# A fused conv-attention and routed-feed-forward kernel: the first routed step gets its own copy of the code, and TensorE gets products of zeros in three places

## The chip, the cores and the metric

The kernel runs on one core of a Trainium2 chip. The metric is the device time of one execution in microseconds (us). Before the change it is 262.25 us, the median of three runs (262.20 to 262.34). The core has engines that run their own instruction streams and meet at semaphores: TensorE (PE; PEld is its weight load), VectorE (DVE), ScalarE (ACT), GpSimd (POOL) and SyncE (SP, which here issues DMAs).

## The reference

The input x is 4 x 64 x 32 x 32, fp32. Two blocks follow each other, each with a residual addition.

1. x += conv attention of the channel norm of x: for each pixel, softmax over its 7 x 7 neighbourhood of q.k plus a relative bias, then the weighted sum of v.
2. t += the routed block of the token norm of t, with 4096 tokens as 4 batches of 1024:

```
def step(h, p):
    op = argmax(h[0, 0, :NOPS])
    q, k, v = h @ wq[op], h @ wk[op], h @ wv[op]
    y = (softmax(q k^T * scale) v) @ wo[op]
    h = where(am[op], y, h)
    z = relu(h @ w1[op] + b1[op]) @ w2[op] + b2[op]
    h = where(fm[op], z, h)
out = scan(step, x, 33 steps)
```

Both masks am and fm depend on the step and on op, and op on the data. A step with both masks off leaves h as it is. Step 0 has fm on and am off for every op.

## The kernel before, in words

**Conv part (0 to 95 us).** Sixteen blocks of queries are worked off in a software pipeline in a loop: scores, exponentials, transposes and the mix. It is not touched.

**Second norm (89 to 105 us).** The tokens are four chunks of 512 columns, j = 0 to 3. For each chunk `centre(j)` (TensorE, L334) subtracts the mean; `square` on ScalarE writes the squares and copies the centred chunk (L708, L710); `variance(1, j)` is four small products on TensorE (L343); `root` on ScalarE (L714) and `inverse` on VectorE (L960) make the reciprocal deviation; `spread(1, j)` (TensorE, L352) spreads it over the partitions; `scale` on VectorE (L966) writes the chunk of h2 and raises `h_ready`. Two rules tie the chunks: `variance(1, j)` with j of 2 or more waits for `h_ready` of j - 1, and each engine works in the order of its program. On TensorE that order is centre(3), variance(1,1), spread(1,0), spread(1,1), variance(1,2), then `load_next()` of the routing, then variance(1,3), spread(1,2), spread(1,3).

**Routing.** Every engine but GpSimd has the same routing code. `load_next` (L176 to L190) waits for the decided op, reads it and a table entry into registers (two register loads, L181 and L184, and arithmetic), and so knows the next step that does anything, with its two masks am and fm. `run` (L207) is a loop over such steps. Each turn is an event: an If on am around `attention`, an If on fm around `feed_forward` (both in `section`, L194), and `load_next`. When a mask is 0, the compare-and-branch of L194 is taken and jumps over the body. In this input there are two events: a feed-forward alone, then attention with a feed-forward.

**feed_forward on TensorE (L651).** For the chunks t = 0 to 3, `up(t, c)` is two products of 64 rows by 512 columns side by side (L660), c = 0 and 1 for the halves of the hidden layer; ScalarE and VectorE each apply bias and relu to one half (L898, L1188); `down(t)` is four products (L674); ScalarE stores the chunk to h2 (L904), after it has also waited for `summed` of 4, that is for GpSimd's four additions of x and h2 (L322) that follow the norm; VectorE adds up (L1195). The order is up(0,0), up(0,1), up(1,0), up(1,1), down(0), up(2,1), up(2,0), down(1), the transposed row of the next decision, up(3,1), up(3,0), down(2), down(3). up(0,*) needs the first chunk of h2, up(1,*) waits for all four.

**attention on TensorE (L529).** Folded weights (L537, L539), `twice(0)` (L546), `queries` (L556), `twice(1)` (L546), then `tile_scores(0)` and `tile_scores(1)` (L582), `values` (L563), and from there 32 tiles in a pipeline of scores, exponentials (L832), transposes (L594) and mixes (L608). tile_scores(0) and (1) wait for parts that ScalarE and VectorE split off after `twice` (L813, L1094). ScalarE copies the values out of PSUM at L824.

`idle_in` is a tile of zeros. Before the change it is used for five products at the very start (L359, L367).

Of the kernel before, what the change touches and what calls it, by code (L numbers as in the profile page):

```python
# [24 lines left out]
ALU = mybir.AluOpType  # L25
# [3 lines left out]
P = 128  # L29
# [25 lines left out]
def build(nc, x, w_qk, w_q, w_v, bias_tables, key_onehot, masks, ident, mean_mat, spread_mat, iotas,  # L55
          attn_mask, ffn_mask, attn_pack, ffn_w1, ffn_pack, out):
    with ExitStack() as ctx:
# [96 lines left out]
        def routing(eng):  # L154
# [9 lines left out]

            name = eng.engine.name
            op, entry, step, cur, last, stride, am, fm, n_att, n_ffn, event = (
                eng.alloc_register(f"{name}_{k}")
                for k in "op entry step cur last stride am fm n_att n_ffn event".split())
            for reg in (n_att, n_ffn, event, cur):  # L170
                eng.reg_mov(reg, 0)

# [3 lines left out]
            def load_next():  # L176
# [12 lines left out]
                eng.reg_add(cur, step, 1)  # L189
                eng.reg_alu(cur, cur, NB, op=ALU.min)  # L190

            def run_event(attention, feed_forward):
                def section(mask, work, done):
                    with eng.If(eng.snap(mask, min_val=0, max_val=2) > 0):  # L194
                        work(eng.snap(n_att, min_val=0, max_val=NB),
                             eng.snap(n_ffn, min_val=0, max_val=NB),
                             eng.snap(event, min_val=0, max_val=NB),
                             eng.snap(eng.snap(step, min_val=0, max_val=NB - 1) * NOPS
                                      + eng.snap(op, min_val=0, max_val=NOPS - 1)))
                        eng.reg_add(done, done, 1)  # L200

                section(am, attention, n_att)
                section(fm, feed_forward, n_ffn)
                eng.reg_add(event, event, 1)
                load_next()

            def run(attention, feed_forward):  # L207
                eng.reg_mov(last, step)

                with eng.Fori(step, NB, stride):
                    run_event(attention, feed_forward)
                    eng.reg_alu(stride, step, last, op=ALU.subtract)
                    eng.reg_mov(last, step)
# [116 lines left out]
        def _(pe):  # L331
# [5 lines left out]
            def variance(k, j):  # L337

                pe.wait_ge(S["squared"], 4 * k + j + 1)
                if j >= 2:  # L340
                    pe.wait_ge(S["h_ready" if k else "normed"], j - 1)
                for s in range(4):
                    mm = nc.tensor.matmul(ps[32 * s:32 * s + 32, 4 + 2 * (j % 2), 0:P], mean_w[:, P:P + 32],  # L343
                                          sq[:, j * 512 + P * s:j * 512 + P * s + P], start=True, stop=True)
                mm.then_inc(S["var_ready"], 1)

            def spread(k, j):

                pe.wait_ge(S["inv_ready"], 4 * k + j + 1)
                for odd in range(2):  # L350
                    for r in range(2):
                        mm = nc.tensor.matmul(ps[:, 4 + 2 * (j % 2) + r, P * odd:P * odd + P],  # L352
                                              spread_w[C * r:C * r + C, odd, :],
                                              sq[C * r:C * r + C, j * 512:j * 512 + P], start=True, stop=True)
                mm.then_inc(S["spread_ready"], 1)

            pe.wait_ge(S["idle_set"], 1)
            for i in range(3):
# [156 lines left out]
            pe.wait_ge(S["mixed"], NPAIR)  # L515
            centre(3)
            variance(1, 1)
            spread(1, 0)
            spread(1, 1)
            variance(1, 2)  # L520
            load_next, run, sections = routing(pe)
            load_next()
# [6 lines left out]
            def attention(a, f, ev, row):  # L529
# [87 lines left out]
                pe.wait_ge(S["fold_a"], a + 1)  # L617
                queries(0, 0)
                twice(1, 6)
                tile_scores(0)  # L620
                tile_scores(1)
                pe.wait_ge(S["fold_d"], a + 2)
# [671 lines left out]
```

## Time and profile before

| | us |
|---|---|
| median of three runs | 262.25 |
| the profiled execution | 261.88 |
| its span, first to last instruction | 260.0 |
| TensorE busy in the span | 230.6 |
| VectorE, ScalarE, GpSimd busy | 170.7, 160.2, 39.5 |
| mean granted TensorE clock, share of full | 0.954 |

In the timelines a row is: start, duration, engine, line, operation, what is written and read, shapes, count, and in brackets the idle time before it with what ended it. Instructions that only an engine's sequencer works off (branches, register loads) are not in timelines or busy times; the view by source line names them with a q behind the engine, PEldq for TensorE's sequencer.

### The profile page before, as it was taken

How to read it: one execution, taken by the hardware profiler on the slowest of the kernel's cores; microseconds unless marked ns; L12 is line 12 of the kernel's file. 1: busy time of each engine (PE TensorE's matmuls, PEld its weight loads, DVE VectorE, ACT ScalarE, POOL GpSimd, SP SyncE). 2: the span in 40 equal slices, each digit the busy share in tenths (PEclk: the TensorE clock that was granted, in tenths of full speed). 3: DMA queues.
4: the chain of work that ended last, by engine and by line, in shares of the span. 5: the costliest groups of instructions: out<-in, count | busy, mean ns of one | idle time of the engine just before them, and what ended most of it. 6: DMA issues, size and time to landing. Idle time of an engine off the chain costs nothing.

```text
span 260.0 us, 5251 instructions
## 1 busy us (share of the span) xinstructions
PE 230.6 (89%) x1794; PEld 156.5 (60%) x1795; DVE 170.7 (66%) x312; ACT 160.2 (62%) x297; POOL 39.5 (15%) x66
## 2 busy tenths in 40 slices
PE   7879963999999996499869999999999999998992
PEld 3247623787777744233247687887877777777320
DVE  0279937677778736146385999898687666871652
ACT  1928753366666784045456997879877776663541
POOL 9800042454444100700000000000000000000000
PEclk9999997799999996579989999999999999999999
DMA  6850000000000010000100000000000000000006
GB/s 167 186 108 1 4 0 1 0 3 0 0 0 0 0 31 0 10 0 3 43 0 0 3 0 0 3 0 3 0 3 0 3 0 3 0 3 0 0 16 149
DMA packets 3304, 4.80 MB, mean 18 GB/s; under 512 B 1041, under 2 KB 2257, under 8 KB 3282
## 3 DMA queue, kind: packets, MB, share of 16 engines
q1 hardware_dynamic: 2758, 3.86, 6.6%
q10 hardware_dynamic: 524, 0.64, 1.1%
q8 instruction: 15, 0.25, 0.4%
q14 instruction: 7, 0.06, 0.1%
HBM read 3.45 MB, written 1.05 MB: 17 GB/s over the span
## 4 chain that ended last, share of the span: by engine, by line
PE 75%; ACT 9%; DVE 7%; issue 6%; ACTq 2%; POOL 0%; DVEq 0%; POOLq 0%
PE ps L594 11%; PE ps L608 11%; PE ps L582 8%; PE ps L660 7%; PE ps L435 7%; PE ps L674 6%; PE ps L467 5%; PE ps L456 5%; ACT arena L883 4%; PE ps L446 2%; PE ps L410 2%; PE ps L334 2%; PE ps L563 2%; DVE arena L996 2%; PE ps L352 2%
## 5 line engine op out<-in xcount | busy, mean ns | idle before, releaser
L883 ACT COPY arena<-ps 128x1024 f32<-128x1024 f32 x32 | 32.4, 1011 | 20.4 <-PE ps L594 19.4
L582 PE MATMUL ps<-h_st,g_st 128*128 128x512 f32 x128 | 39.5, 431 | 2.6 <-DVE h_st L1094 2.3
L1107 DVE TENSOR_REDUCE negmax<-ps 128x1 f32<-128x1024 f32 x32 | 38.7, 1219 | 3.8 <-PE ps L582 3.6
L832 ACT ACTIVATE pr<-ps,negmax 128x1024 f32<-128x1024 f32 x32 | 35.8, 1119 | 4.0 <-DVE negmax L1107 3.7
L594 PE MATMUL ps<-eye,pr 128*128 128x128 f32 x256 | 33.7, 275 | 2.7 <-ACT arena L883 2.3
L594 PEld LDWEIGHTS ps<-eye,pr 128*128 128x128 f32 x256 | 28.6, 140 | 11.1 <-issue 5.0
L608 PE MATMUL ps<-arena,vk 128*64 128x128 f32 x512 | 31.5, 276 | 1.1 <-ACT arena L883 1.1
L608 PEld LDWEIGHTS ps<-arena,vk 128*64 128x64 f32 x512 | 27.6, 137 | 3.8 <-issue 2.3
L766 ACT ACTIVATE prob<-ps,negmax 128x308 f32<-128x308 f32 x32 | 16.3, 513 | 21.0 <-DVE negmax L1007 21.0
L582 PEld LDWEIGHTS ps<-h_st,g_st 128*128 128x128 f32 x128 | 22.2, 193 | 11.3 <-DVE h_st L1094 3.5
L1117 DVE TENSOR_SCALAR pr<-pr,rinv 128x1024 f32<-128x1024 f32 x32 | 24.1, 753 | 1.1
L435 PE MATMUL ps<-arena,q_st 128*128 (+1 forms) x64 | 20.7, 446 | 1.7 <-POOL q_st L295 1.7
L660 PE MATMUL ps<-h,w1d 64*128 64x512 f32 x64 | 18.4, 712 | 3.4 <-issue 3.4
L898 ACT ACTIVATE arena<-ps,w2p 128x512 f32<-128x512 f32 x16 | 11.0, 688 | 15.1 <-PE ps L660 15.1
L1007 DVE TENSOR_REDUCE negmax<-ps 128x2 f32<-128x616 f32 x16 | 12.8, 799 | 7.4 <-PE ps L435 7.4
L456 PE MATMUL ps<-eye,prob 128*103 128x128 f32 x96 | 14.4, 286 | 2.9 <-DVE prob L1015 2.9
L1188 DVE TENSOR_SCALAR arena<-ps,w2p 128x512 f32<-128x512 f32 x16 | 11.6, 746 | 7.1 <-PE ps L660 6.9
L295 POOL TENSOR_TENSOR q_st<-arena,ones_c 128x128 f32<-128x128 f32 x32 | 12.2, 402 | 24.3 <-ACT arena L758 22.5
L776 ACT COPY prob_t<-ps 103x384 f32<-103x384 f32 x32 | 13.7, 481 | 3.1 <-PE ps L456 2.4
L302 POOL TENSOR_TENSOR v_st<-arena,ones_c 128x308 f32<-128x308 f32 x16 | 11.2, 701 | 25.9 <-PE ps L446 25.9
L674 PE MATMUL ps<-arena,w2p 128*64 128x512 f32 x64 | 15.1, 602 | 0.0
L1114 DVE RECIPROCAL rinv<-rowsum 128x1 f32<-128x1 f32 x32 | 5.1, 161 | 14.8 <-ACT pr L832 14.2
(110 smaller groups left out, 335.7 us busy)
## 6 DMA issues: line engine op xcount, KB each, us to landing
arena<-in_key_onehot SPq DMA_DIRECT2D x4, 361.0 KB, 6.2
out<-tabs SPq DMA_DIRECT2D x8, 128.0 KB, 2.3
x<-in_x SPq DMA_DIRECT2D x2, 256.0 KB, 3.9
x<-in_x ACTq DMA_DIRECT2D x2, 256.0 KB, 5.2
w1d<-in_ffn_w SPq DMA_DIRECT2D x4, 64.0 KB, 2.1
w2p<-in_ffn_pack SPq DMA_DIRECT2D x2, 65.5 KB, 1.9
spread_w<-in_spread_mat SPq DMA_DIRECT2D x4, 32.0 KB, 5.0
mean_w<-in_mean_mat SPq DMA_DIRECT2D x1, 96.0 KB, 2.1
```

Source lines behind the costliest of these rows:

```text
L435: mm = nc.tensor.matmul(ps[:, 2 * xb + h, 0:NKEY], q_st[:, xb, h, :], k_aug[:, bass.ds(2 * h + b2, 1), bass.ds(BR * hb, KR), BC * xb:BC * ...
L456: mm = nc.tensor.transpose(ps[0:CH, 4 + h, c * P:c * P + P], prob[:, pp, h, c * CH:c * CH + CH], eye[:])
L582: mm = nc.tensor.matmul(ps[:, 2 * h + c, :], g_st[:, b2, h, q0:q0 + P], h_st[:, b2, h, part, c * 512:c * 512 + 512], start=(part == 0), st ...
L594: mm = nc.tensor.transpose(ps[:, 4 + c // 4, (c % 4) * P:(c % 4) * P + P], pr[:, n % 2, c * P:c * P + P], eye[:])
L608: mm = nc.tensor.matmul(ps[C * h:C * h + C, 7, cols], vk[:, g // 2, c, C * h:C * h + C], prt[:, g % 2, h, c, cols], start=(c == 0), stop=( ...
L660: mm = nc.tensor.matmul(ps[:, set0 + 2 * h + c, :], w1d[C * h:C * h + C, c * P:c * P + P], h2[C * h:C * h + C, t * 512:t * 512 + 512], sta ...
L674: mm = nc.tensor.matmul(ps[C * h:C * h + C, set0 + first, :], w2p[:, c * C:c * C + C], hid[t % 2][:, 2 * h + c, :], start=(i == 0), stop=( ...
L766: ins = nc.scalar.activation(prob[:, pp, h, 0:NKEY], ps[:, 2 * pp + h, 0:NKEY], ACT.Exp, bias=negmax[:, pp, h:h + 1], accum_out=rowsum[:, ...
L832: nc.scalar.activation(pr[:, n % 2, :], ps[:, 2 * (n % 2):2 * (n % 2) + 2, :], ACT.Exp, bias=negmax[:, 0, n % 2:n % 2 + 1], accum_out=rows ...
L883: nc.scalar.copy(prt[:, n // 8 % 2, n % 2, :, q0:q0 + P], ps[:, 4:6, :].rearrange("p b (c q) -> p (b c) q", c=4)).then_inc(S["s_pt"], 1)
L1107: nc.vector.tensor_reduce(negmax[:, 0, n % 2:n % 2 + 1], ps[:, 2 * (n % 2):2 * (n % 2) + 2, :], mybir.AxisListType.XY, ALU.max, negate=Tru ...
L1117: nc.vector.tensor_scalar(pr[:, n % 2, :], pr[:, n % 2, :], rinv[:, 0, n % 2:n % 2 + 1], None, ALU.mult).then_inc(S["s_prob"], 1)
```

## The change

Three parts.

1. `run` first computes `alone` from the two masks (2 when fm is on and am is off, otherwise 0). If it is on, a second copy of `feed_forward` is worked, with its own `load_next`, ahead of the loop. The loop stays as it was.
2. `keep_busy(bank, n)` issues n products of `idle_in` with 256 columns into a PSUM bank that nothing reads then. There are three calls: 3 products before spread(1,0), with a wait for `centre_copied` of 5 ahead of them; 3 products behind spread(1,1); and 4 products between twice(1) and tile_scores(0) of attention.
3. The body of `section` becomes `do_section`; that moves nothing.

```diff
             def run(attention, feed_forward):
+
+                eng.reg_alu(alone, am, 1, op=ALU.logical_shift_left)
+                eng.reg_alu(alone, fm, alone, op=ALU.bitwise_and)
+                eng.reg_alu(alone, fm, alone, op=ALU.subtract)
+                with eng.If(eng.snap(alone, min_val=0, max_val=2) > 0):
+                    do_section(feed_forward, n_ffn)
+                    eng.reg_add(event, event, 1)
+                    load_next()
                 eng.reg_mov(last, step)
...
+            def keep_busy(bank, n):
+                for i in range(n):
+                    nc.tensor.matmul(ps[:, bank, 0:256], idle_in[:, 0:P], idle_in[:, 0:256],
+                                     start=True, stop=True)
...
             variance(1, 1)
+            pe.wait_ge(S["centre_copied"], 5)
+            keep_busy(0, 3)
             spread(1, 0)
             spread(1, 1)
+            keep_busy(0, 3)
             variance(1, 2)
             load_next, run, sections = routing(pe)
             load_next()
...
                 twice(1, 6)
+                keep_busy(0, 4)
                 tile_scores(0)
```

The order of instructions on TensorE from the last spread of the norm on, before (L352 is the spread, L194 the branch on am, L537 attention's first product):

```order
L352 MATMUL ps<-sq,spread_w 128x128 [waits inv_ready]
L352 MATMUL ps<-sq,spread_w 128x128 x3
L208 ISA
L211 UNCONDITIONAL_BRANCH
L194 COMPARE_AND_BRANCH
L195 ISA
L533 ISA
L534 ISA [waits aw_loaded]
L537 MATMUL ps<-wa 64x64 [waits h_ready]
```

And of the change, where L363 is the spread, L215 the new branch, L680 the first product of the feed-forward's copy:

```order
L363 MATMUL ps<-sq,spread_w 128x128 [waits inv_ready]
L363 MATMUL ps<-sq,spread_w 128x128 x3
L212 REGISTER_ALU
L213 REGISTER_ALU
L214 ISA
L215 COMPARE_AND_BRANCH
L193 ISA
L673 ISA
L678 ISA [waits fw_loaded]
L680 MATMUL ps<-h2,w1d 128x512 [waits h_ready]
```

Behind the norm's last spread now stands the feed-forward, where attention stood; with am off, the branch of L194 jumped over attention, and the branch of L215 is not taken with `alone` on.

At the end of the copy, on TensorE, the next `load_next` ends at L189, and attention (L556 is its first product) follows; before, the loop's branch L211 led back to its top:

```order
L189 ISA
L215 UNCONDITIONAL_BRANCH
L219 ISA
L222 UNCONDITIONAL_BRANCH
L202 COMPARE_AND_BRANCH
L193 ISA
L552 ISA
L553 ISA [waits aw_loaded]
L556 MATMUL ps<-wa 64x64 [waits h_ready]
```

The first event leaves the loop, and the second one enters it from above.

## Rows read from the trace of the kernel before

**Rows 1.** Busy time by stretch: length, PE, PEld, DVE, ACT, POOL, clock, DMA.

```profile
14.00:18.00 4.00, 2.72 (x34) 1.39 (x32) 3.02 (x5) 1.77 (x4) 0.00 (x0) 1.00 0.60 120
...
96.00:100.00 4.00, 2.44 (x33) 1.36 (x32) 3.48 (x5) 1.73 (x5) 0.00 (x0) 1.00 0.12 33
110.00:113.62 3.62, 3.62 (x10) 1.46 (x8) 1.83 (x3) 1.58 (x3) 0.21 (x1) 0.50 0.01 2
130.00:134.00 4.00, 1.83 (x8) 0.67 (x4) 3.77 (x7) 2.43 (x5) 0.00 (x0) 1.00 0.00 0
134.10:137.50 3.40, 3.40 (x12) 3.01 (x13) 2.35 (x3) 1.21 (x2) 0.00 (x0) 0.50 0.00 0
107.74:125.90 18.16, 18.04 (x65) 5.96 (x65) 8.11 (x14) 7.62 (x12) 2.47 (x3) 0.84 0.02 6
239.90:255.12 15.22, 15.16 (x67) 4.78 (x65) 9.30 (x16) 7.58 (x12) 0.00 (x0) 1.00 0.12 28
```

**Rows 2.** Timeline of the second norm and the feed-forward's start.

```profile
96.22 0.43 PE L343 MATMUL ps<-sq,mean_w 128*32 128x128 f32 x8
97.08 0.72 PE L352 MATMUL ps<-sq,spread_w 64*128 64x128 f32 x8 [0.43 <-DVE sq L960]
97.99 0.63 DVE L966 TENSOR_TENSOR h<-xc,ps 128x512 f32<-128x512 f32 x1
...
101.06 0.66 PE L343 MATMUL ps<-sq,mean_w 128*32 128x128 f32 x8 [1.86 <-issue]
...
102.17 0.95 DVE L960 RECIPROCAL sq<-sq 128x128 f32<-128x128 f32 x1 [1.56 <-ACT sq L714]
103.18 1.23 PE L352 MATMUL ps<-sq,spread_w 64*128 64x128 f32 x8 [0.31 <-DVE sq L960]
104.52 0.69 DVE L966 TENSOR_TENSOR h<-xc,ps 128x512 f32<-128x512 f32 x1 [0.85 <-PE ps L352]
105.29 4.92 POOL L322 TENSOR_TENSOR tabs<-x,h 128x512 f32<-128x512 f32 x4 [20.05 <-DVE h L966]
107.75 4.64 PE L660 MATMUL ps<-h,w1d 64*128 64x512 f32 x10 [3.35 <-issue]
...
110.19 0.75 DVE L1188 TENSOR_SCALAR arena<-ps,w2p 128x512 f32<-128x512 f32 x1 [4.99 <-PE ps L660]
```

**Rows 3.** By source line, sequencers: durations in ns min/median/max, first and last start.

```profile
L194 PEldq COMPARE_BRANCH  x2: 82/1917/3752, 103.4 to 107.3; - x2
L194 DVEq COMPARE_BRANCH  x2: 50/59/68, 106.8 to 109.8; - x2
L171 PEldq MOVE  x3: 29/29/37, 98.8 to 99.0; - x3
L211 ACTq COMPARE_BRANCH  x1: 54/54/54, 127.4 to 127.4; - x1
L194 ACTq COMPARE_BRANCH  x1: 40/40/40, 127.7 to 127.7; - x1
```

**Rows 4.** Timeline of the second feed-forward, from its first product on.

```profile
239.92 3.70 PE L660 MATMUL ps<-h,w1d 64*128 64x512 f32 x16
241.37 3.05 DVE L1188 TENSOR_SCALAR arena<-ps,w2p 128x512 f32<-128x512 f32 x4
243.55 1.94 PE L674 MATMUL ps<-arena,w2p 128*64 128x512 f32 x8
245.54 0.69 ACT L904 ACTIVATE h<-ps,w2p 128x512 f32<-128x512 f32 x1 [1.18 <-PE ps L674]
```

**Rows 5.** Timeline of attention's start.

```profile
129.50 1.13 PE L546 MATMUL ps<-h,twice_w 64*128 64x512 f32 x4
...
132.64 1.20 PE L582 MATMUL ps<-h_st,g_st 128*128 128x512 f32 x4 [2.01 <-DVE h_st L1094]
134.09 2.07 PE L582 MATMUL ps<-h_st,g_st 128*128 128x512 f32 x4 [0.25 <-DVE h_st L1094]
138.69 1.01 ACT L824 COPY vk<-ps 128x1024 f32<-128x1024 f32 x1 [2.29 <-PE ps L563]
```

More of the change, by code:

```diff
@@ L166, in routing @@
             name = eng.engine.name
-            op, entry, step, cur, last, stride, am, fm, n_att, n_ffn, event = (
+            op, entry, step, cur, last, stride, am, fm, alone, n_att, n_ffn, event = (
                 eng.alloc_register(f"{name}_{k}")
-                for k in "op entry step cur last stride am fm n_att n_ffn event".split())
+                for k in "op entry step cur last stride am fm alone n_att n_ffn event".split())
             for reg in (n_att, n_ffn, event, cur):
@@ L190, in load_next, with do_section @@
                 eng.reg_alu(cur, cur, NB, op=ALU.min)
+            def do_section(work, done):
+                work(eng.snap(n_att, min_val=0, max_val=NB),
+                     eng.snap(n_ffn, min_val=0, max_val=NB),
+                     eng.snap(event, min_val=0, max_val=NB),
+                     eng.snap(eng.snap(step, min_val=0, max_val=NB - 1) * NOPS
+                              + eng.snap(op, min_val=0, max_val=NOPS - 1)))
+                eng.reg_add(done, done, 1)
             def run_event(attention, feed_forward):
@@ L194, in section @@
                     with eng.If(eng.snap(mask, min_val=0, max_val=2) > 0):
[L195 to L200, printed above, removed]
+                        do_section(work, done)
                 section(am, attention, n_att)
```

## The prediction

> **What bounds the kernel now.** I read the slices of the page first, for where the granted clock falls; then the busy times by stretch around those places; then the timeline of the norm; and last the view by source line, because a timeline does not show what a sequencer does. TensorE is busy for 230.6 of 260 us, so the time lies on its chain, and the change works on two places of it.
>
> The first is the second norm and the feed-forward behind it. In 96 to 100 us TensorE works 2.44 of 4.00 us at the full clock [rows 1]. Just before 100 us the granted clock goes from 1.00 to 0.50 (2.4 to 1.2 GHz), and it comes back at 113.6, after a stretch in which the engine was busy throughout [rows 1]. Meanwhile chunk 3 of the norm is finished at 104.52 + 0.69 = 105.21, but the feed-forward's first product starts only at 107.75, put down to "issue" [rows 2]. The sequencers say why: one compare-and-branch on TensorE, the one that jumps over attention, takes 3752 ns from 103.4 on; on VectorE 2.8 us pass from the first such branch (106.8) to what stands behind the jump (a second branch at 109.8, after a register move) [rows 3]. VectorE's first relu is at 110.19 [rows 2], 0.4 behind the second branch, and could not be earlier whatever TensorE did. The two feed-forwards are the same code: the first takes 107.74 to 125.9 at a mean clock of 0.84, its last product ending at about 125.8, the second takes 239.9 to 255.1 at 1.00 [rows 1].
>
> The Trainium skill, page "Runtime: NRT & Kernel Launch", section "Instruction fetch mechanics", says that a taken branch to code that is not yet loaded must wait for a DMA of that code, while straight code is fetched ahead. The 3752 ns agree [rows 3].
>
> The second place is attention's start. In 130 to 134 us TensorE works 1.83 of 4.00 us, and from 134.1 to 137.5 it runs at 0.50 although it is then busy throughout [rows 1].
>
> **The norm with fillers.** One pair of feed-forward products (512 columns, side by side) takes 3.70 / 4 = 0.92 us with its tail, 0.86 in the stream [rows 4]; fp32 of 256 columns is half of that, 0.43, so three fillers are 1.28 us and four 1.71. The wait for `centre_copied` holds nothing up, since ScalarE copied that chunk before 94 us. The first three stand where spread(1,0) is next. The variance before them starts at 96.22, its passes are through at about 96.5, so they end at 97.75, and spread(1,0) starts there and not at 97.08 [rows 2]. It ends at 98.47, and the scale behind it starts at 98.6 and not at 97.99 [rows 2]: +0.6 us. This is on the path. variance(1,2) waits for this scale, and behind it TensorE's sequencer does its `load_next` (first move at 98.8 [rows 3]), so variance(1,3), which started 101.06 - 98.8 = 2.26 us after that move [rows 2, 3], goes from 101.06 to 101.65. Queued behind the fillers are only these products. The second three run from 98.75 to 100.05 beside VectorE's scales and TensorE's own `load_next`; they move variance(1,2) to 100.05. From a variance's start to its reciprocal's end are 102.17 + 0.95 - 101.06 = 2.06 us [rows 2], so chunk 2's is through at 102.1, before chunk 3's begins at 102.5. So they cost nothing; without the cover of `load_next` they would cost 1.28. variance(1,3) at the full clock is 0.43 and not 0.66 [rows 2], which gives back 0.23: spread(1,3) moves from 103.18 to 103.55. As bounds for all this I take 0 and 1.3 us later, the whole of the first fillers.
>
> **Does the clock hold?** This is the uncertain part. With the fillers, 96 to 100 is full. The four microseconds behind them are not: from 99.9 to 103.9 I count 0.15 of filler, two variances (0.43 each), one spread (0.72) and 0.35 of the next, 2.1 of 4.0. Stretches with 2.44 and 1.83 were followed by a fall, one with 2.72 was not [rows 1]. So I expect that the clock does not fall at 100 but at about 103.4, and then, because feed-forward products follow without a gap, that it is back after about 3.4 us, which is how long the shortest slow stretch lasted [rows 1]. Then spread(1,3) takes 1.23 us as before [rows 2] and the last scale is at 103.55 + 1.34 = 104.89 to 105.58, 0.37 later than before.
>
> **The jump.** Behind spread(1,3) TensorE now has three register instructions, a branch that is not taken, and the feed-forward. Before, the branch began 0.2 behind the start of the spread (103.4), and the products began 107.75 - 107.38 = 0.37 behind the end of the second branch (107.3 + 0.08) [rows 2, 3]. With two instructions more that is 103.55 + 0.2 + 0.2 + 0.1 + 0.37, about 104.4; the spread's passes end at 104.6, and up(0,0) starts there, as it needs only chunk 0. The 3.75 us are gone and what is late next is VectorE. Its branch came 106.8 - 104.52 = 2.3 behind the start of the last scale, because its `load_next` stands there [rows 2, 3], and its first relu 110.19 - 109.8 = 0.4 behind the second branch: 104.89 + 2.3 + 0.1 + 0.4 = 107.7. Relus take 0.76 each (3.05 / 4 [rows 4]), so two are done at 109.2.
>
> Four pairs of up are 3.42 us at full and 6.85 at half clock. From 104.6 to 106.8 at half clock 1.1 of the 3.42 is done, and the rest ends at 109.1. In the second feed-forward down(0) starts at 243.55 and all ends at 255.06, 11.5 later [rows 1, 4]. So down(0) at 109.1, with both relus just in time, gives an end at 120.6 where it was 125.8: **-5.2 us**. GpSimd's four additions begin 0.08 behind the last scale and take 4.92 [rows 2], so to 110.6; the first store is due 245.54 - 243.55 = 2.0 after down(0) [rows 4], at 111.1, so they are hidden by 0.5 us.
>
> **The loop.** The jump back to the loop's top is gone: on ScalarE the branch at 127.4 ended at 127.44 and the next one began at 127.7 with a move before it [rows 3], some 0.2 to 0.25 us. This is on the path, since attention's start hangs on ScalarE. **-0.2 us**, with 0 and 0.3 as bounds. SyncE's DMA of attention's weights is issued after the decision in the middle of the feed-forward, and moves forward with it.
>
> **Attention's start.** twice(1) ends at 130.6 and tile_scores(0) starts at 132.64, waiting for VectorE [rows 5]: 2.0 us of room for 1.71 of fillers. Then the clock stays up in either case of the first part. tile_scores(1) takes 1.20 and not 2.07; the eight products of values then start 0.87 earlier and take about 1.75 (8 products of 128 columns, 0.21 each) where they ended with ScalarE's copy at 138.69. That copy comes at 134.09 + 1.20 + 1.75 + 0.1 = 137.15: **-1.5 us**. The transposes of tile 0 wait for it, and the whole pipeline behind it moves along. Bounds: 0, if the fillers came late enough to push tile_scores(0) by as much, and 1.6.
>
> **Sum.** 5.2 + 0.2 + 1.5 = 6.9. The profiled execution goes from 261.88 to 255.0; the median of the runs lies 0.37 above the profiled one, which gives 255.3.
>
> **The rivals.**
>
> *A, the clock never falls* in norm and feed-forward. Then spread(1,3) takes 0.72, the last scale starts at 104.38, up(0,0) at 104.4, VectorE's relus at 107.2, down(0) at 107.95, the end at 119.5; GpSimd is through at 110.07 and the first store was due at 109.95, which costs 0.2 with the latency of the semaphore: 119.7, or -6.1. Sum 6.1 + 0.2 + 1.5 = 7.8, time **254.4**. For it: my count of 2.1 could be low, and the longest idle time left is about 1.1 us. Against it: the rows on 96 to 100 and on 130 to 134.
> The Trainium skill, page "TensorE: Matmul & The Clock Gate", section "Why this matters for your kernels", sends the clock down only after a gap of some microseconds without any matmul, and by it A would be the outcome. The trace speaks against it: in 96 to 100 the engine was busy for 2.44 us with no long gap, and the clock fell [rows 1].
>
> *C, the clock falls at 103.4 and stays down until 110.* Then 2.8 of the 3.42 us of up are done by 110.2 and the rest by 110.8; the end is at 122.3, -3.5, sum 5.2, time **257.0**. For it: the slow stretch before lasted 13.6 us. Against it: TensorE was far from full in most of that one.
>
> *D, the copy is fetched cold as well.* Straight code could stall where it runs past what is loaded. If each engine paid at the entry of the copy what the jump cost, the first part gives only what the clock gives: up at 107.8 at full clock, the end at 122.9, sum 2.9 + 0.2 + 1.5, time **257.6**. Against it: TensorE streams new code all through attention with no idle time put down to it.
>
> *E, slower.* Before, the loop's top with the start of attention was already loaded when the loop came back (0.25 us); now attention stands behind new code. If ScalarE and VectorE had to fetch there, once for entering it and once more within its start, as they had behind the jump, that is 2.8 - 0.25 + 2.8 = 5.3 us, while D's loss takes away the gain of the jump, and the clock falls as before: 262.25 + 5.3 - 1.5 = **266**. It decides from one such stall on: 2.55 - 1.5 is still 1.0 slower when nothing else is gained. Against it: code in sequence has no taken branch.
>
> *F, the change does not do what it says:* the masks give `alone` = 0 and the copy is jumped over. The trace rules it out: the first event jumped over attention and did the feed-forward.
>
> **How the numbers follow.** Forecast 0.50, A 0.25, C 0.11, D 0.08, E 0.03, the rest 0.03 spread around them. The predicted time is 255.3. The range goes from 254.0 (A with the bound of its small terms) to 257.4 (C and most of D); below it and above it lie about 0.08 each. A measurement of this kernel tells 0.2% (0.5 us) from no change. Every case but E is well below 261.7, so faster 0.96, within 0.2% 0.01, slower 0.03.
>
> **What would show it.** In the profile after: no compare-and-branch above 0.2 us on TensorE ahead of the first L680, and this product near 104.6; VectorE's first relu near 107.7; the clock at 1.00 until about 103.4, 0.50 to 106.8, then 1.00 into attention; first fillers 96.5 to 97.75, spread(1,0) at 97.75; down(0) near 109.1, the last product of the first feed-forward near 120.6; ScalarE's copy of the values 11.2 us behind that (12.9 before); from there to the end of the span the same time as before. The prediction is wrong if a branch on any engine still takes microseconds, or if the clock in this part is at 0.50 for longer than 4 us or not at all.

## The result, and the profile after

The change makes the kernel faster: the median is 255.41 us (four runs, 254.52 to 256.15) where 262.23 us was measured before beside it; the ratio is 0.9756, with a 95% interval of 0.9716 to 0.9797. The prediction was 255.3 in a range of 254.0 to 257.4. The profiled execution takes 256.12 us with a span of 254.3. One execution of the changed kernel in a later run took 329.18 us at a mean granted clock of 0.653; it is left out of all that is compared below.

Slices of the page after; the digits are the granted clock in tenths (9 is 90% or more), to be held against the falls of before at slices 6 and 7, 15 to 17 and 20:

```profile
PEclk9999998599999999799999999999999999999997
```

Two of the three falls remain, the one in the conv part and one slice in the norm; attention's is gone. The lowered last slice lies behind TensorE's last product.

Busy time by stretch after (length, PE, PEld, DVE, ACT, POOL, clock, DMA). The first goes from the norm's last centre product (from the second of its two records, as in all that follows) to the first feed-forward's last product, and will be called the **norm length**; before it was 95.70 to 125.79, 30.09 us.

```profile
96.28:121.81 25.53, 23.80 (x137) 10.30 (x136) 14.16 (x22) 11.45 (x20) 4.95 (x4) 0.93 0.03 9
100.57:104.57 4.00, 2.27 (x30) 1.21 (x28) 2.20 (x4) 1.79 (x3) 0.00 (x0) 1.00 0.02 4
104.57:107.98 3.41, 3.41 (x14) 2.01 (x16) 1.15 (x2) 0.89 (x3) 1.33 (x2) 0.50 0.00 0
```

Before, the slow stretch began just before 100 us and lasted 13.6 us [rows 1]; now it begins at 104.57 and lasts 3.41. The timeline below is the part that answers to [rows 2] and [rows 4]. All of this execution is 0.58 us later than before's at the norm's last centre product (95.75 against 95.17). The conv part ahead of it is not touched by the change, and a second trace of the same kernel has this product at 94.76. Weight loads (PEld) are left out of the timelines, and dots stand for other rows:

```profile
97.16 1.56 PE L370 MATMUL ps<-idle_in 128*128 128x256 f32 x6
...
98.66 1.16 PE L363 MATMUL ps<-sq,spread_w 64*128 64x128 f32 x16
99.49 1.28 DVE L986 TENSOR_TENSOR h<-xc,ps 128x512 f32<-128x512 f32 x2 [0.84 <-PE ps L363]
99.75 1.56 PE L370 MATMUL ps<-idle_in 128*128 128x256 f32 x6
...
102.65 0.43 PE L354 MATMUL ps<-sq,mean_w 128*32 128x128 f32 x8 [0.98 <-issue]
...
104.54 1.23 PE L363 MATMUL ps<-sq,spread_w 64*128 64x128 f32 x8 [0.69 <-DVE sq L980]
...
105.56 4.81 PE L680 MATMUL ps<-h,w1d 64*128 64x512 f32 x16
105.89 0.69 DVE L986 TENSOR_TENSOR h<-xc,ps 128x512 f32<-128x512 f32 x1 [0.85 <-PE ps L363]
106.65 4.95 POOL L333 TENSOR_TENSOR tabs<-x,h 128x512 f32<-128x512 f32 x4 [20.83 <-DVE h L986]
...
108.72 2.73 DVE L1208 TENSOR_SCALAR arena<-ps,w2p 128x512 f32<-128x512 f32 x4 [2.14 <-PE ps L680]
...
110.30 1.94 PE L694 MATMUL ps<-arena,w2p 128*64 128x512 f32 x8
...
112.28 0.69 ACT L924 ACTIVATE h<-ps,w2p 128x512 f32<-128x512 f32 x1 [1.18 <-PE ps L694]
...
118.15 3.65 PE L694 MATMUL ps<-arena,w2p 128*64 128x512 f32 x16
```

The feed-forward's first product (L680) starts 1.0 us behind the start of the last spread; before it was 4.6 [rows 2]. TensorE works on the four ups, at half clock until 107.98, and down(0) (L694 at 110.30) starts when they are through; VectorE's second relu ended 0.2 us before (108.72 + 2 x 0.68 = 110.1). The branches, to be held against [rows 3]:

```profile
L215 PEldq COMPARE_BRANCH  x1: 78/78/78, 104.9 to 104.9; - x1
L215 DVEq COMPARE_BRANCH  x1: 54/54/54, 108.3 to 108.3; - x1
```

Where the jump took 3752 ns, the branch that is not taken takes 78. And attention's start, against [rows 5]:

```profile
126.22 1.99 PE L370 MATMUL ps<-idle_in 128*128 128x256 f32 x8
...
128.50 1.19 PE L601 MATMUL ps<-h_st,g_st 128*128 128x512 f32 x4 [0.28 <-DVE h_st L1114]
...
129.94 1.19 PE L601 MATMUL ps<-h_st,g_st 128*128 128x512 f32 x4 [0.25 <-DVE h_st L1114]
...
132.96 1.02 ACT L844 COPY vk<-ps 128x1024 f32<-128x1024 f32 x1 [0.70 <-PE ps L582]
```

tile_scores(1) takes 1.19 in place of 2.07. From the feed-forward's last product to this copy (the **attention length** below) are 11.15 us where it was 12.89. From the copy to the end of the span nothing changed: 121.32 us now, 121.35 before.

So the two lengths hold the whole change: 30.09 to 25.53, and 12.89 to 11.15, together 6.3 us, less the 0.58 of the late start: 5.7 of the 5.76 us between the two profiled executions (261.88 and 256.12).

### The profile page after: what moved, and what is told of

Its sections match the earlier page's. It is cut to its first block, busy times and chain, and to the rows that moved or that the text cites. A ratio compares the mean times of both kernels' runs of the same rounds, so it can differ in the third digit from the quotient of the medians.

```text
span 254.3 us, 5286 instructions
## 1 busy us (share of the span) xinstructions
PE 231.9 (91%) x1814; PEld 158.1 (62%) x1815; DVE 170.4 (67%) x312; ACT 160.3 (63%) x297; POOL 39.5 (16%) x66
## 4 chain that ended last, share of the span: by engine, by line
PE 79%; ACT 7%; DVE 7%; issue 4%; DVEq 1%; POOL 0%; ACTq 0%; POOLq 0%
PE ps L613 12%; PE ps L627 11%; PE ps L601 8%; PE ps L451 7%; PE ps L680 6%; PE ps L694 6%; PE ps L483 5%; PE ps L472 5%; ACT arena L903 4%; PE ps L462 2%; PE ps L426 2%; PE ps L345 2%; PE ps L375 2%; PE ps L363 2%; DVE arena L1016 2%
## 5 line engine op out<-in xcount | busy, mean ns | idle before, releaser
L601 PE MATMUL ps<-h_st,g_st 128*128 128x512 f32 x128 | 38.6, 423 | 0.9 <-DVE h_st L1114 0.5
L680 PE MATMUL ps<-h,w1d 64*128 64x512 f32 x64 | 16.6, 651 | 0.0
L313 POOL TENSOR_TENSOR v_st<-arena,ones_c 128x308 f32<-128x308 f32 x16 | 11.2, 701 | 26.4 <-PE ps L462 26.4
L472 PEld LDWEIGHTS ps<-eye,prob 128*103 128x103 f32 x96 | 11.5, 174 | 6.1 <-issue 6.1
L694 PE MATMUL ps<-arena,w2p 128*64 128x512 f32 x64 | 15.1, 602 | 0.0
L451 PEld LDWEIGHTS ps<-arena,q_st 128*128 128x128 f32 x64 | 11.4, 198 | 5.6 <-issue 2.8
```

The costliest lines, as they stand in the source:

```text
L451: mm = nc.tensor.matmul(ps[:, 2 * xb + h, 0:NKEY], q_st[:, xb, h, :], k_aug[:, bass.ds(2 * h + b2, 1), bass.ds(BR * hb, KR), BC * xb:BC * ...
L472: mm = nc.tensor.transpose(ps[0:CH, 4 + h, c * P:c * P + P], prob[:, pp, h, c * CH:c * CH + CH], eye[:])
L601: mm = nc.tensor.matmul(ps[:, 2 * h + c, :], g_st[:, b2, h, q0:q0 + P], h_st[:, b2, h, part, c * 512:c * 512 + 512], start=(part == 0), st ...
L680: mm = nc.tensor.matmul(ps[:, set0 + 2 * h + c, :], w1d[C * h:C * h + C, c * P:c * P + P], h2[C * h:C * h + C, t * 512:t * 512 + 512], sta ...
L694: mm = nc.tensor.matmul(ps[C * h:C * h + C, set0 + first, :], w2p[:, c * C:c * C + C], hid[t % 2][:, 2 * h + c, :], start=(i == 0), stop=( ...
```

## The experiments

Each table row gives the median, the ratio to the kernel before as run beside it with its 95% interval, and from its one trace the norm length with the granted clock's slow stretches in it, and the attention length. The kernel before had medians of 261.35 to 261.79 beside the runs below and of 262.23 beside the first, and single executions from 259.91 to 263.54, so kernels that were not run together are compared by their ratios.

| label | us | ratio | norm length (slow) | attention length |
|---|---|---|---|---|
| before | 262.25 | | 30.09 (13.65) | 12.89 |
| the change | 255.41 | 0.9756 [0.9716, 0.9797] | 25.53 (3.41) | 11.15 |
| d1_change_again | 254.46 | 0.9752 [0.9713, 0.9792] | 24.43 (none) | 11.16 |
| e1_copy_only | 256.96 | 0.9818 [0.9778, 0.9858] | 25.97 (6.83) | 12.66 |
| e2_fillers_only | 260.98 | 0.9961 [0.9930, 0.9991] | 30.17 (6.83) | 11.31 |
| e3_copy_norm | 255.02 | 0.9745 [0.9703, 0.9787] | 24.43 (none) | 12.02 |
| e4_copy_attn | 255.61 | 0.9769 [0.9730, 0.9808] | 25.93 (6.83) | 11.15 |
| d2_hold | 254.31 | 0.9736 [0.9704, 0.9768] | 23.97 (none) | 11.15 |
| d3_early_route | 256.67 | 0.9797 [0.9752, 0.9842] | 27.17 (6.83) | 11.16 |
| d4_jump | 260.68 | 0.9974 [0.9949, 1.0000] | 30.23 (6.83) | 10.98 |
| d5_short_jump | 254.04 | 0.9710 [0.9663, 0.9758] | 24.67 (none) | 10.96 |
| d6_tensor_route | 252.82 | 0.9664 [0.9628, 0.9700] | 22.51 (none) | 11.14 |
| d7_no_attn | 253.84 | 0.9696 [0.9653, 0.9739] | 22.51 (none) | 12.53 |
| d8_no_norm | 253.86 | 0.9697 [0.9651, 0.9744] | 23.40 (3.41) | 11.16 |

**The three parts apart.** `e1_copy_only` has no products of zeros, `e2_fillers_only` has them and no copy, `e3_copy_norm` leaves out the four in attention, `e4_copy_attn` the six in the norm.

```diff
--- the change, e1_copy_only; e4_copy_attn has the first half alone, e3_copy_norm the second
-            pe.wait_ge(S["centre_copied"], 5)
-            keep_busy(0, 3)
...
-            keep_busy(0, 3)
...
-                keep_busy(0, 4)
--- the change, e2_fillers_only
-                eng.reg_alu(alone, am, 1, op=ALU.logical_shift_left)
-                eng.reg_alu(alone, fm, alone, op=ALU.bitwise_and)
-                eng.reg_alu(alone, fm, alone, op=ALU.subtract)
-                with eng.If(eng.snap(alone, min_val=0, max_val=2) > 0):
-                    do_section(feed_forward, n_ffn)
-                    eng.reg_add(event, event, 1)
-                    load_next()
```

> The copy of the feed-forward alone, no products of zeros anywhere. Theory (the norm fillers buy nothing, because the clock falls anyway in the norm and comes back under the feed-forward's own products; attention's four are worth 1.5 us): the clock falls near 100 and is back near 107, the last product of the first feed-forward lies 5.2 us earlier than before; attention's start runs at half clock as before. Time 262.2 - 5.2 - 0.2 = 256.8. Rival (the fillers are what shortens the slow stretch): the clock stays down until 110 or later, only 3.3 us are gained, time 258.9 or more.

> All three groups of products of zeros, without the copy. Theory: the compare-and-branch of 3.75 us stays, TensorE idles behind the norm, so the clock goes down there as before and the first feed-forward starts slow; the norm is up to 0.4 us later; only attention's 1.5 us are gained: 261.1. Rival (the norm fillers hold the clock through norm and feed-forward): 2.9 us more are gained, 258.2.

> The change without the four products in attention. Theory: attention's start has its slow stretch again, 1.5 us more than the change: 256.9, and the copy of the values again 12.7 us behind the first feed-forward's last product. Rival (in the new place in time the clock would not fall there anyway): as the change, 255.4.

> The change without the six products in the norm. Theory: same time as the change within 0.3 us, 255.4: the spread is 0.6 earlier, the slow stretch begins earlier and ends under the feed-forward. Rival (the norm fillers carry a share): the slow stretch is longer than 7 us and the time 257 or more.

Stretches of e1_copy_only (norm length, and from there on the two in which the granted clock is 0.50), and of e3_copy_norm (norm length, and the one at 0.50 in attention):

```profile
95.36:121.33 25.97, 22.50 (x125) 8.82 (x124) 14.29 (x22) 11.47 (x20) 4.93 (x4) 0.87 0.03 9
102.03:108.86 6.83, 6.22 (x20) 3.17 (x22) 3.20 (x5) 2.45 (x4) 4.11 (x4) 0.50 0.01 2
129.34:132.75 3.41, 3.28 (x11) 2.90 (x12) 2.38 (x4) 1.21 (x2) 0.00 (x0) 0.50 0.02 5
```

```profile
96.72:121.15 24.43, 22.55 (x137) 9.60 (x136) 14.17 (x22) 11.46 (x20) 4.96 (x4) 1.00 0.03 9
127.50:130.91 3.41, 3.07 (x7) 2.49 (x8) 2.63 (x4) 0.47 (x1) 0.00 (x0) 0.50 0.02 5
```

The copy alone gives 4.1 of the norm length's 4.6 us (30.09 to 25.97), and 0.23 in attention's (12.89 to 12.66, with the slow stretch still there). The loop's share came as expected; the norm length gained 1.1 us less than the 5.2 expected, with a slow stretch of 6.83 us. The time of 256.96 hides that: the 256.8 expected was counted from 262.2, and the kernel before beside this run had 261.79. Without the copy the products of zeros leave the norm length as it was (30.17), because the jump stays: the slow stretch is 6.83 us where it was 13.65, but the feed-forward's first product starts 12.81 us behind the last centre product (109.63 - 96.82) where it was 12.05 (107.75 - 95.70). The branch of e2_fillers_only on TensorE's sequencer, shortest, median and longest of two:

```profile
L202 PEldq COMPARE_BRANCH  x2: 82/1900/3719, 105.3 to 109.2; - x2
```

e3_copy_norm was a miss: 256.9 was expected, 255.02 measured. Its attention's slow stretch is back as expected, and the length is 0.87 longer; but in its norm the clock never fell. That could not come from the four products it leaves out, which stand behind. Its profiled execution is its slowest all the same (256.37): the last centre product is at 96.72, 1.43 us later than in the second trace of the change, so the part ahead of the norm differs between executions by more than the norm does. By its ratio e3_copy_norm is no slower than the change.

e4_copy_attn came out in time as the theory had it, 255.61 (0.9769). Its timeline prices the six products in the norm:

```profile
97.47 0.63 DVE L983 TENSOR_TENSOR h<-xc,ps 128x512 f32<-128x512 f32 x1
...
102.45 1.22 PE L363 MATMUL ps<-sq,spread_w 64*128 64x128 f32 x8 [0.82 <-DVE sq L977]
```

From the last centre product (95.19) the last spread starts 7.26 us later, in the change 8.26 (104.54 - 96.28). So the six products hold the norm up by 1.00 us, not by the 0.6 that this run's theory had; the norm length is 0.4 us longer without them all the same, because the slow stretch is 6.83 us in place of 3.41.

**The same kernel again.** No edit.

> The changed kernel as it is, again. Theory: where the edges of the slow and fast stretches of TensorE's clock fall against the work differs from execution to execution (in the six traces so far the first edge lies between 38.7 and 43.1 us), so its times spread over some 1.5 us, and a second trace shows the slow stretch of the norm at another place, or not at all; from the norm's last centre product to the first feed-forward's last product are 25.5 us where the clock fell (first trace) and near 24.5 where it did not. Rival: the spread comes from the loads or the conv part, and these two lengths are the same in every trace.

Stretches and timeline of this trace, in which the clock stays up through the norm:

```profile
95.29:119.72 24.43, 22.54 (x137) 9.60 (x136) 14.17 (x22) 11.45 (x20) 4.95 (x4) 1.00 0.03 9
99.58:103.58 4.00, 2.26 (x30) 1.20 (x28) 2.19 (x4) 1.78 (x3) 0.00 (x0) 1.00 0.01 4
```

```profile
104.35 3.70 PE L680 MATMUL ps<-h,w1d 64*128 64x512 f32 x16
...
107.22 2.73 DVE L1208 TENSOR_SCALAR arena<-ps,w2p 128x512 f32<-128x512 f32 x4 [2.15 <-PE ps L680]
...
108.12 1.94 PE L694 MATMUL ps<-arena,w2p 128*64 128x512 f32 x8
...
110.20 0.69 ACT L924 ACTIVATE h<-ps,w2p 128x512 f32<-128x512 f32 x1 [1.41 <-POOL tabs L333]
```

The same instructions took 24.43 us here and 25.53 in the first trace. In the four microseconds that end where the clock fell there (104.57, 8.29 behind the last centre product) TensorE was busy for 2.27 us, and at the same place here (103.58) for 2.26, and the clock stayed up. The theory holds: whether the clock falls there differs from execution to execution, and the norm length with it, by 1.1 us. The slow stretch of the conv part, which this change does not touch, also lies elsewhere in each (41.94 to 48.76 before, 43.13 to 49.95 and 40.50 to 47.33 in the two traces of the change); it is 10.24 us long in the traces of e3_copy_norm, d3_early_route and d4_jump, and e2_fillers_only and e3_copy_norm have one more of 3.41 us at 18.6 and 18.3. Of the 2.09 us between the two profiled executions of the change (256.12 and 254.03), 0.99 stand already at the last centre product. The executions of this run are 253.96 to 255.57.

**The jump.** In `d4_jump` a skipped copy of attention stands ahead of the copy of the feed-forward; in `d5_short_jump` what is skipped is another feed-forward.

```diff
                 with eng.If(eng.snap(alone, min_val=0, max_val=2) > 0):
+                    with eng.If(eng.snap(am, min_val=0, max_val=2) > 0):
+                        do_section(attention, n_att)
                     do_section(feed_forward, n_ffn)
```

> The change, with a skipped copy of attention between the new branch and the copy of the feed-forward: same work, but the jump over attention is back, in straight code outside the loop. Theory (the jump over code that was not fetched is what cost 3.75 us): one compare-and-branch of 3 to 4 us on TensorE, some 2.7 us on ScalarE and VectorE, the clock down behind it, 30 us from the last centre product to the first feed-forward's last product; time 260.5. Rival (what cost was the loop's entry, and the copy is free of it): 256 or less.

> As the experiment with the skipped attention, but what is skipped between the new branch and the copy is a second feed-forward, which is short: a taken branch over a small distance. Theory (a jump costs only where it leaves the code that is already fetched): no compare-and-branch above 0.4 us on any engine, time 255.2 as the change with 0.2 for the branch. Rival (any taken branch stalls): 3 to 4 us on TensorE again, time 260.5.

The view by source line of d4_jump, its timeline at the feed-forward, and the same source line of d5_short_jump:

```profile
L216 PEldq COMPARE_BRANCH  x1: 3892/3892/3892, 104.7 to 104.7; - x1
L216 DVEq COMPARE_BRANCH  x1: 67/67/67, 107.5 to 107.5; - x1
```

```profile
104.09 0.71 PE L365 MATMUL ps<-sq,spread_w 64*128 64x128 f32 x8 [0.69 <-DVE sq L982]
...
108.94 3.78 PE L682 MATMUL ps<-h,w1d 64*128 64x512 f32 x8 [4.13 <-issue]
111.06 0.69 ACT L920 ACTIVATE arena<-ps,w2p 128x512 f32<-128x512 f32 x1 [6.49 <-PE ps L682]
```

```profile
L216 PEldq COMPARE_BRANCH  x1: 225/225/225, 104.1 to 104.1; - x1
```

With the long jump back in straight code the whole gain of the copy is gone (norm length 30.23, time 260.68 against an expected 260.5); with the short one the branch takes 225 ns and the norm length is 0.24 more than d1's. It is the distance of the jump that costs, not a taken branch, nor the loop. That the engines wait for their code is borne out by the DMA queues that carry instructions. In 103 to 111 us they show, as packets, MB and share of the 16 engines' time, before, in the change, in d4_jump and in d5_short_jump, in this order:

```profile
q8 instruction: 2, 0.03, 2.1%
q14 instruction: 4, 0.03, 1.5%
```

```profile
q8 instruction: 1, 0.02, 1.0%
```

```profile
q8 instruction: 3, 0.05, 3.1%
q14 instruction: 3, 0.02, 1.1%
```

```profile
q14 instruction: 1, 0.01, 0.3%
```

Six packets of code stand where the long jump is, in both kernels that have it, and one where it is not.

The time of d5_short_jump was a miss downward: 255.2 was expected, and all four executions lie between 253.76 and 254.37. In its one trace the clock stayed up in the norm, which gives about 1 us; whether it did in all four, and why, is open.

**Placing the products of zeros, and the routing's load.** `d2_hold` puts them where TensorE was seen to wait: one ahead of spread(1,0), one ahead of spread(1,1), four behind variance(1,2), two ahead of spread(1,3). `d3_early_route` also moves `load_next` on TensorE and on VectorE, and has one product in place of the four. `d6_tensor_route` moves it on TensorE alone and has four products in the norm:

```diff
--- the change, d6_tensor_route
             centre(2)
+            load_next, run, sections = routing(pe)
+            load_next()
             mix(1, 15)
...
             pe.wait_ge(S["centre_copied"], 5)
-            keep_busy(0, 3)
+            keep_busy(0, 1)
             spread(1, 0)
+            keep_busy(0, 1)
             spread(1, 1)
-            keep_busy(0, 3)
             variance(1, 2)
-            load_next, run, sections = routing(pe)
-            load_next()
+            keep_busy(0, 1)
             variance(1, 3)
+            keep_busy(0, 1)
             spread(1, 2)
```

> Products of zeros placed where TensorE waits and never ahead of a product whose operands are ready: one ahead of each spread of chunks 0 and 1, four beside the routing's load, two ahead of the last spread (eight in place of six). Theory: the clock cannot fall in the norm wherever the edges lie, and spread(1,0) is 0.6 us earlier: 23.8 to 24.0 us from the norm's last centre product to the first feed-forward's last product, time 254.0 to 254.5. Rival (what ends last is VectorE's routing load and not TensorE): as the change in its better traces, 254.8 or more.

> As d2_hold, and the routing's load moves: on TensorE from ahead of variance(1,3) to behind centre(2), on VectorE from behind the last scale to behind scale(1,1). Theory: on the path of the norm stands TensorE's load (2.3 us, beside 0.7 of other work), and behind it VectorE's; both now lie where the sequencers wait. Last scale some 2 us earlier, 0.4 us of that lost because mix(1,15) starts late: 22.5 us from the last centre product to the first feed-forward's last product, time 252.9. Rival: GpSimd's four additions or ScalarE's table load take the place of the wait, and it is 253.8 or more.

> The version that the runs point to. TensorE's routing load goes behind centre(2), VectorE's stays behind the last scale (its move delayed both reciprocals by 1.5 us in d3_early_route), and no product of zeros stands ahead of the last spread (there two of them at half clock took 2.07 us of the path); one each ahead of spread(1,0), spread(1,1), variance(1,3) and spread(1,2). Theory: 1.3 us less than d2_hold from the last centre product to variance(1,3), of which 0.4 is lost to GpSimd's additions and 0.3 to the late mix: 23.1 us from the last centre product to the first feed-forward's last product, time 253.7. Rival (four products are too few, the clock falls in some executions): spread as wide as the change's, median above 254.3.

d2_hold came as expected: norm length 23.97, clock at 1.00, 254.31 us, executions from 253.97 to 255.07. The 0.46 us less than d1's 24.43 is what the placing saves: the last spread starts 7.81 us behind the last centre product (103.86 - 96.05) where the change has 8.26. Without any products in the norm it is 7.26 (e4_copy_attn), so here they still cost 0.55.

d3_early_route was a miss in the wrong direction, 256.67. Its timeline:

```profile
101.95 1.76 DVE L982 RECIPROCAL sq<-sq 128x128 f32<-128x128 f32 x2 [1.47 <-ACT sq L736]
...
104.12 2.07 PE L370 MATMUL ps<-idle_in 128*128 128x256 f32 x4
...
106.12 1.23 PE L363 MATMUL ps<-sq,spread_w 64*128 64x128 f32 x8
```

The move aimed at 252.9. VectorE's routing load stood ahead of both reciprocals, which could start only at 101.95; the clock fell in the wait, at 102.66, and stayed low for 6.83 us; and the two products of zeros ahead of the last spread, ready or not, then took 2.07 us at half clock with the spread queued behind them. A product of zeros is work like any other: it costs nothing only as long as the wait that it fills is there.

With VectorE's load back in its place and no product of zeros ahead of the last spread, d6_tensor_route is the best version: 252.82 us, ratio 0.9664 [0.9628, 0.9700], 0.9 us less than expected, and its six executions agree within 0.41 us (252.61 to 253.02). Its norm length as a stretch, and its timeline:

```profile
95.80:118.31 22.51, 22.17 (x133) 8.75 (x132) 14.35 (x22) 11.11 (x18) 4.95 (x4) 1.00 0.04 9
```

```profile
100.25 0.43 PE L354 MATMUL ps<-sq,mean_w 128*32 128x128 f32 x8
...
102.98 3.70 PE L682 MATMUL ps<-h,w1d 64*128 64x512 f32 x16
```

variance(1,3) starts 100.25 - 95.80 = 4.45 us behind the last centre product, in d2_hold 5.74: TensorE's routing load had been on the path for 1.3 us. The two kernels without products in the norm say the same: 4.10 in d8_no_norm, where the load is moved (100.06 - 95.96), and 5.37 in e4_copy_attn, where it is not (100.56 - 95.19).

**What the products of zeros give.** The last two leave out of d6_tensor_route the four in attention and the four in the norm.

> d6_tensor_route without the four products in attention. Theory: attention's start gets its slow stretch back, 12.0 to 12.7 us from the first feed-forward's last product to ScalarE's copy of the values in place of 11.15: time 253.7 to 254.3. Rival (those products buy nothing, as the equal medians of the change with and without them would say): 252.8.

> d6_tensor_route without the four products in the norm. Theory: the clock falls in the norm in most executions, and comes back under the feed-forward: 24.0 to 24.6 us from the last centre product to the first feed-forward's last product in place of 22.5, time 254.3 to 254.9. Rival (with TensorE's routing load gone from the norm, it is short enough that the clock holds without them): 252.8, or less by the 0.1 to 0.3 that they may cost.

Both are 1.0 us slower than d6_tensor_route by the medians. In d7_no_attn the slow stretch is back (125.98 to 129.40) and the attention length is 12.53, as expected. In d8_no_norm the clock was low from 102.33 to 105.75 and the norm length was 23.40, less than the 24.0 expected, and so was its time. Its executions spread from 252.52 to 254.97, and the fastest has a mean granted clock of 0.985 where the others have 0.968 to 0.975, so in that one the clock seems to have held without them; it has no trace. The intervals of these three ratios overlap, but the traces agree with the medians. For the four in attention the record is mixed: here 1.0 us by the medians and 1.39 by the attention length, in e3_copy_norm 0.87 by the length and nothing by the ratio, from e1_copy_only to e4_copy_attn 1.51 and 1.35.

## Why the prediction was right, and where not

**The number: near, in part by luck.** The terms add up to 6.9 us. The two lengths hold 6.3 in the first trace of the change and 7.4 in the second (5.66 + 1.73), and the last centre product, with the conv part the same, lies anywhere from 95.19 to 96.82 in the traces. That 255.3 lies 0.1 beside the median of four is not the prediction's precision; it took the kernel before to be known to 0.5 us, from three runs, where its executions spread over 3.6.

**The jump: right.** Its going was said to let up(0,0) start right behind the last spread, and it did. d4_jump puts the stall back and the gain of the copy goes. By itself the copy is worth 4.1 us in the norm length. VectorE was named as next in line, and down(0) was to start when both of its first relus are done. It was not a limit: down(0) starts when the ups are through, in d1 at 108.12, while the second relu ends there at 107.22 + 2 x 0.68 = 108.6. By the program the first half of down(0) needs only the first relu.

**The loop and attention's start: right.** 12.9 to 11.2 was forecast, 12.89 to 11.15 measured; e1 and e4 split it into 0.23 for the loop and 1.51 for the four products. Without the four products attention's slow stretch was there in all four traces (before, e1, e3, d7), but not at the same instructions, so their worth is 0.9 to 1.5 us.

**The first fillers: under-sized.** They were taken at 0.43 us each, from the feed-forward's products, 1.28 for three. The first of them starts 98.66 - 97.16 = 1.50 us ahead of the spread. In d6_tensor_route one alone starts 97.31 - 96.68 = 0.63 ahead of it, so each further one does take 0.43, and what was left out is 0.2 us once per group. The scale behind spread(1,0) was to be 0.6 us later than before and is 0.93 later than in e4_copy_attn (99.49 - 96.28 against 97.47 - 95.19). On before's time axis (0.58 earlier) the last spread starts at 103.96 and not at 103.55; that is most of the difference between the norm length forecast (120.6 - 95.7 = 24.9) and the 25.53 measured. The cover of the second three held, as forecast: chunk 2's reciprocal, which they delay, is through at 103.1, before chunk 3's begins at 103.53.

**The clock: the right outcome for one execution, the wrong idea of it.** The forecast was that it falls at about 103.4 and comes back after 3.4 us; it fell at 104.57 (103.99 on before's axis) and came back after 3.41. But this was argued as something the kernel does. I counted work in stretches around the falls of before and concluded that the change falls into the forecast's case or A or C, each time. The two traces of the change show the forecast's case and A with the same work, and by the prediction's own sign of being wrong (not at 0.50 at all in this part) the second one speaks against it. Its first four runs lie at 254.5 to 254.7 and at 256.1 to 256.2, and the median falls between them; that the norm's slow stretch is what separates them is not shown, since the untraced one at 256.15 has the same mean granted clock (0.980) as those at 254.5 and 254.7, and d1's executions lie in between too. What was called the chances of rivals was in part a share of executions. The count itself was nearly right (2.1 us where 2.33 are busy, 100.48 to 104.48 in the first trace), but d1 shows that 2.27 is followed by a fall and 2.26 by none, so the comparison with 2.44 and 2.72 [rows 1] could not decide it.

**Rival A** is real, and its mechanism held; even its small wait of the first store for GpSimd is there in d1 (110.20, ended by POOL). Its sum gives 261.88 - 7.8 = 254.1 for the profiled execution and d1's is 254.03, but this is luck to 0.4 us: the norm length was to be 119.7 - 95.7 = 24.0 and is 24.43, and the execution had its last centre product 0.41 us earlier than before's. The Trainium skill's rule ("TensorE: Matmul & The Clock Gate", "Why this matters for your kernels"), that it takes a gap of some microseconds without a matmul, gives A; in the first trace the clock fell at 104.57 with 2.27 of 4.00 us busy ahead of it and no idle stretch of TensorE of even 1.1 us in the norm. So the rule does not say when the clock holds.

**C, D, E:** no trace of the change shows a slow stretch beyond 3.41 in the norm and the feed-forward, and no branch in the copy or at attention's entry takes over 0.1 us. One small stall of rival E's kind is there: on VectorE, whose sequencer goes from the first to the second of these two at attention's entry (124.6 + 0.1 to 125.1), 0.41 us pass without anything that it waits for.

```profile
L193 DVEq FUSED_REGOPS  x1: 107/107/107, 124.6 to 124.6; - x1
L1159 DVEq ALU_OP  x1: 45/45/45, 125.1 to 125.1; - x1
```

d4_jump and d5_short_jump do not have it there, and their attention lengths are 0.2 us shorter (10.98 and 10.96). Why it stands there is open. That the copy's code is fetched in time agrees with the Trainium skill, "Runtime: NRT & Kernel Launch", "Instruction fetch mechanics", by which code in sequence is fetched ahead and a taken branch to a place outside of it waits for a DMA; d5_short_jump's 225 ns beside d4_jump's 3892 shows the distance on which it turns.

**The value of the norm's six** was in no term of the prediction, and my theory for the experiments, that they buy nothing, does not stand as it was. In both traces without them and with the copy and the load in its old place (e1, e4) the clock is slow for 6.83 us, with them for 3.41 once (the first trace) and not at all three times (d1, e3, d5); they cost 1.00 us up to the last spread and give back more. Norm lengths with and without: 25.53, 24.43 and 24.43 against 25.93 and 25.97. Ratios: 0.9756 and 0.9752 against 0.9769, and 0.9745 against 0.9818. The gain is between 0.3 and 1.9 us; these runs do not fix it closer.

## What to carry to other kernels

Look for the branches in the view of the sequencers when an engine idles with "issue": here a jump over a long body cost 3.8 us on TensorE and 2.8 on VectorE, and in a straight copy of what comes next no engine stood still for longer than 0.5. Products of zeros that hold TensorE's clock belong where the engine waits, never ahead of a product that could be ready; and before a clock stretch in a trace is made a term of a forecast, a second trace of the same kernel should show that it is always there.

## What the runs showed of the hardware that was not expected

- The place of the clock's fall against the work is not fixed by the program: the same kernel had a slow stretch of 3.41 us in the norm in one trace and none in another, with 2.27 and 2.26 of 4.00 us busy ahead of that place, and its norm length differs by 1.10 us by that. The slow stretch of the conv part was 6.83 us in eleven of the fourteen traces and 10.24 in three.
- The narrowest spread is d6_tensor_route's, 0.41 us in six executions; the change's nine spread over 2.2 us. That the clock holds in the norm of all six is likely but seen in one trace.
- One compare-and-branch over attention took 3719 to 3892 ns on TensorE in three kernels, 225 ns over a feed-forward, and 78 ns when not taken. On VectorE the branch itself takes 67 ns in d4_jump, and its next instruction comes 3 us later.
- Products of zeros (fp32, 256 columns) follow each other at 0.43 us at the full clock, and a group holds up what is behind it by 0.2 us more (0.63 for one, 1.50 for three); at half clock two of them held the spread up by 2.0 us (104.12 to 106.12 in d3_early_route).
